# A decoder layer on one core: the order of work behind the last attention head

## The chip, the cores and the metric

The kernel runs on one core of a Trainium2 chip. The metric is the device time of one execution in microseconds (us), the median over runs. Its engines are TensorE (PE, matrix products, with PEld for its weight loads), VectorE (DVE), ScalarE (ACT), GpSimd (POOL) and SyncE (SP), which here only issues DMAs. They run side by side, each takes its own instructions in program order, and they meet through semaphores.

## The reference, cut to what matters

Batch 8, 128 rows each, width 512. Three blocks, each with a layer norm ahead and a residual behind:

```python
x = x + _L0_attn_ref(_layernorm(x), Wq, Wk, Wv, Wo)                      # causal self-attention, rope
x = x + _L0_xattn_ref(_layernorm(x), ctx_4096, Wq, Wk, Wv, Wo, qn, kn)   # 32 heads, 8 key heads of 128
x = x + _L0_ffn_ref(_layernorm(x), weight_q4, weight_scale, bias)        # one 512x512 product, 4-bit weights

# in _L0_xattn_ref
scores = jnp.einsum('bhgqd,bhkd->bhgqk', qg, k) * scale
probs = jax.nn.softmax(scores.astype(jnp.float32), axis=-1)
out = jnp.einsum('bhgqk,bhkd->bhgqd', probs, v)
...
return out @ Wo
```

## The kernel before

`self_attention` runs first and is not touched. `cross_attention_and_linear` runs the other two blocks. It goes through `STEPS` = 64 steps: key head j = 0 to 7 outside, batch row b = 0 to 7 inside, so step s is head s // 8 and row s % 8. Each step projects keys, values and queries of one row, takes the scores of the four query heads that share the key head, their softmax, the values, and adds the product with this head's slice of Wo to row b of `acc` (the residual stream, tile `x` in the trace). In the last head (j = `LAST` = 7) row b of `acc` is final after its step, so that the linear block's work on finished rows is spread over the steps that follow.

All products are split: a float32 operand is kept as a high part (rounded, `_hi`) and a low part (the rest, `_lo`), and `split_matmuls` issues for each slice three products: high x high, high x low and low x high (line 73). The high part is written by ACT (a copy that rounds), the low part by DVE or POOL (a subtraction), and before, a group of products starts when both parts stand.

The order of work is written out by hand, engine by engine, as calls of small functions that each wait for their semaphores and raise one. Names that matter, with s a step and b a row:

- SP: `probs_out(s)` writes the transposed blocks of the probabilities `p_blocks` to DRAM (L922), `probs_in(s)` reads them back as `pT_raw` in another layout (L930, four DMAs). The eight output rows are stored behind the loop over steps (L974); row b waits for `out_ok`.
- ACT: `probs_high(s)` rounds `pT_raw` into `pT_hi_sb` (L1113), `output_high(s)` rounds the attention output `ps_o` into `oT_hi` (L1124), `xn_high(b)` rounds the transposed normalised row `ps_xn` (L1135, tile `wkv_hi`).
- POOL: `probs_low(s)` subtracts (L1008), `row_rstd(b)` makes the layer norm's reciprocal deviation (L1027, L1029), `row_and_bias(b)` adds the bias to a row (L1037).
- DVE: `residual(s)` adds `ps_y` to `acc` (L1236), `statistics(b)` (L1259, L1261), `normalised(b)` (L1269, tile `raw_wkv`), `xn_low_row(b)` (L1274, tile `wkv_lo`), `output_low(s)` (L1240, tile `oT_lo`), `out_row(b)` adds the linear block's product and the biased row into `y` (L1284, tile `raw_wq`).
- PE: `values(s)` (tile `ps_o`, 6 products), `project_output(s)` (`ps_y`, 12 products), `xn_transposed(b)` (`ps_xn`, 4 transposes, L1396), `linear(b)` (12 products, into `ps_f` for even rows and `ps_q` for odd ones).

`y` has two buffers. `out_row(b)` from row 2 on waits until the store of row b - 2 has landed:

```python
if b >= 2:
    dve.wait_ge(stored[b % 2], 16 * (b // 2))
```

In the loop's last step (s = 63, b = 7) DVE ends with `residual(61)`, `statistics(5)` and `out_row(2)`. SP's program has by then `probs_out(63)` and `probs_in(63)` ahead of the first store.

Of the kernel before, what the change touches and what calls it, by code (L numbers as in the profile page):

```python
# [16 lines left out]
ALU = mybir.AluOpType  # L17
# [51 lines left out]
def split_matmuls(pe, out, parts, start=True, stop=True):  # L69

    terms = [(a, b) for lh, ll, rh, rl in parts for a, b in ((lh, rh), (lh, rl), (ll, rh))]
    for i, (lhsT, rhs) in enumerate(terms):
        mm = pe.matmul(out, lhsT, rhs, start=start and i == 0, stop=stop and i == len(terms) - 1)  # L73
    return mm


# [727 lines left out]
def cross_attention_and_linear(nc, mem, io):  # L804
# [7 lines left out]
    with ExitStack() as ctx:  # L812
# [83 lines left out]
        @block.sync  # L896
        def _(sp):
            def load(raw, name, sem, j):
                sp.dma_start(raw[:].rearrange("p c n -> p (c n)"), io[name][j]).then_inc(sem, 16)

            def queries_keys_out(s):

                sp.wait_ge(q_blocked, s + 1)
                sp.wait_ge(k_blocked, s + 1)
                wait(sp, qT_lo, s - 1)
                sp.dma_start(io["qk_scratch"][s % 2], qk_blocks[:].rearrange("p j x c -> p (j x c)")).then_inc(qk_stored, 16)

            def queries_keys_in(s):

                wait(sp, qT_lo, s - 1)  # L910
                wait(sp, kT_lo, s - 1)
                sp.wait_ge(qk_stored, 16 * (s + 1))
                quadrants = io["qk_scratch"][s % 2].rearrange("(i r) (j x) -> j r i x", i=4, j=4)
                for j in range(4):
                    sp.dma_start(qk_raw[s % 2][R * j:R * j + R].rearrange("p i x c -> p i (x c)"),
                                 quadrants[j]).then_inc(qk_loaded[s % 4], 16)

            def probs_out(s):

                sp.wait_ge(p_blocked, 2 * s + 2)  # L920
                wait(sp, pT_lo, s - 1)
                sp.dma_start(io["p_scratch"][s % 2], p_blocks[:].rearrange("p m g c -> p (m g c)")).then_inc(p_stored, 16)  # L922

            def probs_in(s):

                wait(sp, o_ps, s - 1)
                sp.wait_ge(p_stored, 16 * (s + 1))
                quadrants = io["p_scratch"][s % 2].rearrange("(i r) (j x) -> j r i x", i=4, j=4)
                for j in range(4):
                    sp.dma_start(f32(pT_raw[s % 2][R * j:R * j + R].rearrange("p i t x -> p i (t x)")),  # L930
                                 quadrants[j]).then_inc(p_loaded[s % 4], 16)

            def linear_scales(t):

                for g in range(8):
                    sp.dma_start(scale[16 * g:16 * g + 16, t, :],
                                 io["q4_scale"][8 * t + g:8 * t + g + 1, :].broadcast_to([16, D])).then_inc(scale_in, 16)

            queries_keys_out(0)
            queries_keys_in(0)  # L940
            load(raw_wkv, "x_wkv", wkv_in, 1)
            queries_keys_out(1)
            queries_keys_in(1)
            load(raw_wo, "x_wo", wo_in, 0)
            queries_keys_out(2)
            load(raw_wq, "x_wq", wq_in, 1)
            for s in range(STEPS):
                j, b = divmod(s, B)
                probs_out(s)
                if s + 2 < STEPS:  # L950
                    queries_keys_in(s + 2)
                probs_in(s)
                if s + 3 < STEPS:
                    queries_keys_out(s + 3)
                if b == 2 and j + 2 < XKVH:
                    sp.wait_ge(wkv_lo, 2 * j + 2)
                    load(raw_wkv, "x_wkv", wkv_in, j + 2)
                if b == 3 and j < LAST:
                    sp.wait_ge(wo_lo, j + 1)
                    load(raw_wo, "x_wo", wo_in, j + 1)  # L960
                if b == 5 and j + 2 < XKVH:
                    sp.wait_ge(wq_lo, 2 * j + 2)
                    load(raw_wq, "x_wq", wq_in, j + 2)
                if j + 1 == LAST:
                    if b == 5:
                        sp.wait_ge(wq_lo, 2 * LAST)
                        sp.dma_start(packed, io["q4"].rearrange("t p o -> p t o")).then_inc(packed_in, 16)
                        sp.dma_start(f_bias[:], io["bias"].broadcast_to([P, D])).then_inc(bias_in, 16)
                    if b >= 6:
                        linear_scales(b - 6)  # L970

            for b in range(B):
                sp.wait_ge(out_ok, b + 1)
                sp.dma_start(io["out"][b], y[:, b % 2, :]).then_inc(stored[b % 2], 16)  # L974
            for done in stored:
                sp.wait_ge(done, 16 * B // 2)

        @block.gpsimd
        def _(pool):
# [89 lines left out]
                        row_and_bias(b - 5)  # L1069
            row_rstd(5)  # L1070
            row_and_bias(3)
            probs_low(STEPS - 1)
            row_rstd(6)
            row_and_bias(4)
            row_and_bias(5)
# [5 lines left out]
        def _(act):  # L1081
# [92 lines left out]
            output_high(STEPS - 2)  # L1174
            xn_high(4)
            probs_high(STEPS - 1)
            xn_high(5)
            output_high(STEPS - 1)
            xn_high(6)
            xn_high(7)  # L1180

# [1 line left out]
        def _(dve):  # L1183
# [60 lines left out]
            def linear_bits(b):  # L1244
# [6 lines left out]
                if b in (1, 3):  # L1251
# [2 lines left out]
                    dve.wait_ge(scale_in, 16 * 16)  # L1254
                    dve.scalar_tensor_tensor(weights[h], bits[h], 2.0 / 15.0, scale, ALU.mult, ALU.mult).then_inc(product_ok, 1)

            def statistics(b):
                dve.wait_ge(acc_ok, LAST * B + b + 1)
                dve.bn_stats(stats[:, b, :], acc[:, b, :]).then_inc(stats_ok, 1)  # L1259
                dve.wait_ge(stats_ok, b + 1)  # L1260
                dve.bn_aggr(moments[:, b, :], stats[:, b, :]).then_inc(moments_ok, 1)  # L1261
# [30 lines left out]
            for s in range(STEPS):  # L1292
# [24 lines left out]
                if j == LAST:  # L1317
                    if b >= 2:
                        statistics(b - 2)
                    if b >= 5:  # L1320
                        out_row(b - 5)
            normalised(4)
            output_low(STEPS - 2)
            xn_low_row(4)
            normalised(5)
            out_row(3)
            residual(STEPS - 2)
            statistics(6)
            xn_low_row(5)
            normalised(6)  # L1330
            out_row(4)
            output_low(STEPS - 1)
            xn_low_row(6)
            residual(STEPS - 1)
            statistics(7)
            normalised(7)
            out_row(5)
            xn_low_row(7)
            out_row(6)
# [3 lines left out]
        def _(pe):  # L1343
# [38 lines left out]
            def project_output(s):  # L1382
# [4 lines left out]
                split_matmuls(pe, ps_y[:], [(oT[0][:, g, :], oT[1][:, g, :], wo[0][:, g, :], wo[1][:, g, :])  # L1387
                                            for g in range(XG)]).then_inc(y_ps, 1)

            def xn_transposed(b):  # L1390
                pe.wait_ge(xn_ok, b + 1)
                wait(pe, xn_lo, b)
# [41 lines left out]
            linear(3)  # L1434
            xn_transposed(4)
            project_output(STEPS - 2)
            xn_transposed(5)
            linear(4)
            values(STEPS - 1)
            xn_transposed(6)  # L1440
            project_output(STEPS - 1)
            linear(5)
            xn_transposed(7)
            linear(6)
            linear(7)


def build(nc, io):
# [65 lines left out]
```

## Time and profile before

| | us |
|---|---|
| time before, median of 3 runs | 992.04 |
| the 3 runs | 990.35, 992.80, 992.04 |
| span of the profiled execution, first to last instruction | 989.3 |
| PE busy | 927.3 (94%) |
| DVE busy | 742.3 (75%) |
| ACT busy | 604.4 (61%) |
| POOL busy | 568.9 (58%) |

The profiled execution is one of its own; its span is given, and what lies ahead of its first and behind its last instruction is not printed. The median of the runs stands 2.7 us above the span. A busy share is an average over the whole execution: PE is near full in the loop over steps, and in the last two of 40 slices its digit falls from 9 to 7. The views used are the chain of waits that ended last (each piece with its start and length, the engine and the tile it writes), and the timelines of single engines.

### The profile page before, as it was taken

The numbers are of one execution on the slowest core, as the hardware profiler recorded it, in microseconds if no ns is written. First come the engines' busy times: TensorE is split into PE (matmuls) and PEld (weight loads), VectorE is DVE, ScalarE is ACT, GpSimd is POOL, SyncE is SP. The second block draws the span as 40 slices with busy tenths as digits, with TensorE's granted clock in tenths as the row PEclk, the third lists the DMA queues.
The fourth block names the chain that finished last, engine by engine and source line by source line (L and its number), as shares of the span: only waits on it lengthen the run. The fifth ranks groups of instructions, "written<-read, shape, count | busy, mean of one in ns | idle before, by whom it ended". The sixth has DMA issues, their size and how long they took to land.

```text
span 989.3 us, 17511 instructions
## 1 busy us (share of the span) xinstructions
PE 927.3 (94%) x5484; PEld 797.2 (81%) x5492; DVE 742.3 (75%) x1555; ACT 604.4 (61%) x2226; POOL 568.9 (58%) x593
## 2 busy tenths in 40 slices
PE   5689999769999999999999999999999999999977
PEld 5567777548888888888888888888888888888765
DVE  6678988855877777777777777777777777789964
ACT  1568888615856676665667556765756675575530
POOL 6522322224865685677458656856774686468643
PEclk8799999779999999999999999999999999999999
DMA  5000020006666566557645665665576456654431
GB/s 203 12 12 13 12 87 12 1 1 223 211 219 205 168 209 208 172 167 231 211 149 186 213 210 169 198 209 178 167 236 196 150 175 209 214 170 150 134 117 54
DMA packets 101148, 149.84 MB, mean 151 GB/s; under 512 B 11840, under 2 KB 77376, under 8 KB 98880
## 3 DMA queue, kind: packets, MB, share of 16 engines
q1 hardware_dynamic: 101056, 148.71, 47.2%
q8 instruction: 45, 0.74, 0.3%
q14 instruction: 47, 0.39, 0.1%
HBM read 87.85 MB, written 60.82 MB: 150 GB/s over the span
## 4 chain that ended last, share of the span: by engine, by line
PE 69%; DVE 4%; ACT 1%; POOL 1%; issue 1%; DMA 1%; SPq 0%; DVEq 0%; POOLq 0%
PE ps_kv L73 17%; PE ps_y L73 17%; PE ps_q L73 17%; PE ps_o L73 8%; PE ps_s L73 8%; ACT ps_s L1090 1%; DVE p L1202 1%; PE ps_f L73 1%; DVE neg_max L1190 1%; POOL pT_raw L1008 1%; DVE p_blocks L1206 0%; DVE raw_wkv L1269 0%; DMA out<-raw_wq 0%; DVE kT_lo L1229 0%; DVE f_stats L1259 0%
## 5 line engine op out<-in xcount | busy, mean ns | idle before, releaser
L1090 ACT ACTIVATE ps_s<-ps_s,bias,q_rms 128x256 f32<-128x256 f32 x256 | 136.8, 535 | 139.5 <-DVE bias L1194 139.5
L1001 POOL TENSOR_TENSOR qT_lo<-qk_raw,qT_hi 128x512 fp32r<-128x512 f32 x64 | 84.6, 1322 | 202.6 <-ACT qT_hi L1119 202.6
L1008 POOL TENSOR_TENSOR pT_raw<-pT_raw,pT_hi_sb 128x1024 fp32r<-128x1024 f32 x64 | 154.1, 2408 | 11.9 <-ACT pT_hi_sb L1113 11.6
L1107 ACT ACTIVATE q_squares<-ps_q 128x128 bf16<-128x128 f32 x256 | 67.5, 278 | 112.0 <-DVE qk_blocks L1224 112.0
L73 PE MATMUL ps_y<-wo_hi,oT_hi 128*128 128x512 f32 x256 | 101.7, 397 | 4.9 <-DVE oT_lo L1240 4.9
L73 PE MATMUL ps_q<-wq_lo,xT_hi 128*128 128x512 f32 x256 | 101.4, 396 | 0.0
L73 PE MATMUL ps_q<-wq_hi,xT_lo 128*128 128x512 f32 x256 | 101.1, 395 | 0.0
L73 PE MATMUL ps_y<-wo_lo,oT_hi 128*128 128x512 f32 x256 | 101.1, 395 | 0.0
L1206 DVE STREAM_TRANSPOSE p_blocks<-p 128x512 f32<-128x512 f32 x128 | 91.1, 711 | 13.3
L73 PE MATMUL ps_y<-wo_hi,oT_lo 128*128 128x512 f32 x256 | 101.0, 394 | 0.0
L73 PE MATMUL ps_q<-wq_hi,xT_hi 128*128 128x512 f32 x256 | 100.9, 394 | 0.0
L1236 DVE TENSOR_TENSOR x<-ps_y,x 128x512 f32<-128x512 f32 x64 | 44.2, 691 | 70.4 <-PE ps_y L73 70.3
L1202 DVE TENSOR_TENSOR p<-ps_s,inv 128x512 f32<-128x512 f32 x128 | 88.6, 692 | 4.4
L1190 DVE TENSOR_REDUCE neg_max<-ps_s 128x2 f32<-128x512 f32 x128 | 87.7, 685 | 5.3
L73 PE MATMUL ps_kv<-wkv_hi,cT_hi 128*128 128x256 f32 x256 | 73.7, 288 | 4.1 <-DVE k_sb L1214 4.1
L1224 DVE STREAM_TRANSPOSE qk_blocks<-ps_q 128x512 f32<-128x512 f32 x64 | 45.8, 716 | 42.2 <-PE ps_q L73 41.9
L73 PE MATMUL ps_s<-kT_hi,qT_hi 128*128 128x256 f32 x256 | 72.6, 284 | 2.7 <-DVE kT_lo L1229 1.3
L73 PE MATMUL ps_kv<-wkv_hi,cT_lo 128*128 128x256 f32 x256 | 73.2, 286 | 0.0
L73 PE MATMUL ps_kv<-wkv_lo,cT_hi 128*128 128x256 f32 x256 | 73.1, 286 | 0.0
L73 PE MATMUL ps_kv<-wkv_hi,xT_hi 128*128 128x256 f32 x256 | 73.0, 285 | 0.0
L73 PE MATMUL ps_kv<-wkv_lo,xT_hi 128*128 128x256 f32 x256 | 72.6, 284 | 0.0
L73 PE MATMUL ps_kv<-wkv_hi,xT_lo 128*128 128x256 f32 x256 | 72.5, 283 | 0.0
(217 smaller groups left out, 2940.2 us busy)
## 6 DMA issues: line engine op xcount, KB each, us to landing
p_scratch<-p_blocks SPq DMA_DIRECT2D x64, 512.0 KB, 3.0
pT_raw<-p_scratch SPq DMA_DIRECT2D x256, 128.0 KB, 3.1
qk_scratch<-qk_blocks SPq DMA_DIRECT2D x64, 384.0 KB, 3.5
qk_raw<-qk_scratch SPq DMA_DIRECT2D x256, 96.0 KB, 2.9
raw_wq<-in_x_wq SPq DMA_DIRECT2D x8, 1024.0 KB, 7.8
raw_wo<-in_x_wo SPq DMA_DIRECT2D x8, 1024.0 KB, 7.5
raw_wkv<-in_x_wkv SPq DMA_DIRECT2D x8, 512.0 KB, 5.0
ctx_raw<-in_ctxT SPq DMA_DIRECT2D x8, 256.0 KB, 2.7
```

Source lines behind the costliest of these rows:

```text
L73: mm = pe.matmul(out, lhsT, rhs, start=start and i == 0, stop=stop and i == len(terms) - 1)
L1001: pool.tensor_tensor(qT[1][:].rearrange("p g (i c) -> p g i c", i=4), qk_raw[s % 2][:, :, 0:XG, :].rearrange("p i g c -> p g i c"), f32(qT ...
L1008: pool.tensor_tensor(raw, f32(raw), f32(pT_hi_sb[:].rearrange("p i t x -> p (i t x)")), ALU.subtract).then_inc(pT_lo, 1)
L1090: e = act.activation(scores, scores, ACT.Exp, bias=bias[:, g:g + 1], scale=q_rms[:, s % 4, g:g + 1], accum_out=total[:, g:g + 1])
L1107: i = act.activation(q_squares[:, g, :], ps_q[:, g * XD:(g + 1) * XD], ACT.Square, scale=XD ** -0.5, accum_out=q_mean[:, g:g + 1])
L1190: dve.tensor_reduce(neg_max[:, two], ps_s[h][:].rearrange("p (g k) -> p g k", g=2), AX.X, ALU.max, negate=True).then_inc(max_ok, 1)
L1202: dve.tensor_tensor(p[:, two, :], ps_s[h][:].rearrange("p (g k) -> p g k", g=2), inv[:, two].unsqueeze(2).broadcast_to([P, 2, KV]), ALU.mu ...
L1206: dve.transpose(p_blocks[:, :, two, :], p[:, two, :].rearrange("p g (m r) -> p m g r", r=R)).then_inc(p_blocked, 1)
L1224: dve.transpose(qk_blocks[:, :, 0:XG, :].rearrange("p j x c -> p x j c"), ps_q[:].rearrange("p (g j r) -> p g j r", g=XG, r=R)).then_inc(q ...
L1236: dve.tensor_tensor(acc[:, b, :], ps_y[:], acc[:, b, :], ALU.add).then_inc(acc_ok, 1)
```

## The change

Four edits, all in the last head.

1. SP: the store of rows 0 and 1 moves into the loop, to the head of steps 62 and 63; rows 2 to 7 are stored behind it.
2. PE: the products of the last step with values and with Wo, and the linear product of row 7, are issued with the products of the high part first, which wait for the high part alone; the products of the low part wait for it and come last. The count of products is unchanged.
3. `probs_low(63)`, the low part of the last probabilities, moves from POOL to DVE.
4. Behind the loop the calls are put in another order on PE, DVE and ACT.

```diff
+def high_parts_first(pe, out, parts, low, count, start=True, stop=True):
+
+    for i, (lh, _, rh, rl) in enumerate(parts):
+        pe.matmul(out, lh, rh, start=start and i == 0, stop=False)
+        pe.matmul(out, lh, rl, start=False, stop=False)
+    pe.wait_ge(low, count)
+    for i, (_, ll, rh, _) in enumerate(parts):
+        mm = pe.matmul(out, ll, rh, start=False, stop=stop and i == len(parts) - 1)
     return mm
@@ sync
+            def store(b):
+                sp.wait_ge(out_ok, b + 1)
+                sp.dma_start(io["out"][b], y[:, b % 2, :]).then_inc(stored[b % 2], 16)
...
                 j, b = divmod(s, B)
+                if j == LAST and b >= 6:
+                    store(b - 6)
                 probs_out(s)
...
-            for b in range(B):
-                sp.wait_ge(out_ok, b + 1)
-                sp.dma_start(io["out"][b], y[:, b % 2, :]).then_inc(stored[b % 2], 16)
+            for b in range(2, B):
+                store(b)
@@ gpsimd
             row_and_bias(3)
-            probs_low(STEPS - 1)
             row_rstd(6)
@@ scalar
             probs_high(STEPS - 1)
+            output_high(STEPS - 1)
             xn_high(5)
-            output_high(STEPS - 1)
             xn_high(6)
@@ vector
+            def probs_low(s):
+                dve.wait_ge(pT_hi, s + 1)
+                raw = pT_raw[s % 2][:].rearrange("p i t x -> p (i t x)")
+                dve.tensor_tensor(raw, f32(raw), f32(pT_hi_sb[:].rearrange("p i t x -> p (i t x)")),
+                                  ALU.subtract).then_inc(pT_lo, 1)
...
+            output_low(STEPS - 2)
             normalised(4)
-            output_low(STEPS - 2)
             xn_low_row(4)
             normalised(5)
+            probs_low(STEPS - 1)
             out_row(3)
             residual(STEPS - 2)
+            output_low(STEPS - 1)
             statistics(6)
             xn_low_row(5)
             normalised(6)
             out_row(4)
-            output_low(STEPS - 1)
-            xn_low_row(6)
             residual(STEPS - 1)
             statistics(7)
             normalised(7)
+            xn_low_row(6)
             out_row(5)
@@ tensor
+            def last_values():
+                s = STEPS - 1
+                pe.wait_ge(pT_hi, s + 1)
+                pe.wait_ge(o_lo, s)
+                hi, lo = pT_hi_sb, pT_raw[s % 2]
+                for t in range(2):
+                    for x in range(2):
+                        pe.matmul(ps_o[:], v[s % 5][x][:, t, :], hi[:, :, t, :], start=t == 0 and x == 0, stop=False)
+                pe.wait_ge(pT_lo, s + 1)
+                for t in range(2):
+                    mm = pe.matmul(ps_o[:], v[s % 5][0][:, t, :], lo[:, :, t, :], start=False, stop=t == 1)
+                mm.then_inc(o_ps, 1)
+
+            def last_output():
+                pe.wait_ge(o_hi, STEPS)
+                pe.wait_ge(acc_ok, STEPS - 1)
+                high_parts_first(pe, ps_y[:], ..., o_lo, STEPS).then_inc(y_ps, 1)
+
+            def last_linear():
+                pe.wait_ge(xn_hi, B)
+                pe.wait_ge(out_ok, B - 2)
+                x = xnT[(B - 1) % 2]
+                high_parts_first(pe, ps_f[(B - 1) % 2][:], ..., xn_lo, B).then_inc(f_ps, 1)
...
             project_output(STEPS - 2)
+            last_values()
             xn_transposed(5)
             linear(4)
-            values(STEPS - 1)
+            last_output()
+            linear(5)
             xn_transposed(6)
-            project_output(STEPS - 1)
-            linear(5)
+            linear(6)
             xn_transposed(7)
-            linear(6)
-            linear(7)
+            last_linear()
```

SP's queue at its end, before; `out_0` is the output in DRAM, `p_scratch` and `pT_raw` the round trip of the probabilities of steps 62 and 63:

```order
L922 DMA p_scratch0<-p_blocks 128x1024 [waits pT_lo,p_blocked]
L930 DMA pT_raw0<-p_scratch0 32x4x256 [waits p_stored,b_o_ps]
L930 DMA pT_raw0<-p_scratch0 32x4x256 x3
L922 DMA p_scratch1<-p_blocks 128x1024 [waits pT_lo,p_blocked]
L930 DMA pT_raw1<-p_scratch1 32x4x256 [waits p_stored,b_o_ps]
L930 DMA pT_raw1<-p_scratch1 32x4x256 x3
L974 DMA out_0<-raw_wq 128x512 [waits f_out_ok] x8
```

All eight stores stand behind both round trips.

The same place of SP's queue in the changed kernel:

```order
L952 DMA out_0<-raw_wq 128x512 [waits f_out_ok]
L933 DMA p_scratch0<-p_blocks 128x1024 [waits pT_lo,p_blocked]
L941 DMA pT_raw0<-p_scratch0 32x4x256 [waits p_stored,b_o_ps]
L941 DMA pT_raw0<-p_scratch0 32x4x256 x3
L952 DMA out_0<-raw_wq 128x512 [waits f_out_ok]
L933 DMA p_scratch1<-p_blocks 128x1024 [waits pT_lo,p_blocked]
L941 DMA pT_raw1<-p_scratch1 32x4x256 [waits p_stored,b_o_ps]
L941 DMA pT_raw1<-p_scratch1 32x4x256 x3
L952 DMA out_0<-raw_wq 128x512 [waits f_out_ok] x6
```

One store stands ahead of each of the two round trips, six behind.

DVE before, from `out_row(2)`, the last call of the loop, to `output_low(63)`:

```order
L1284 TENSOR_TENSOR raw_wq<-ps_f,raw_wq 128x512 [waits stored_even,f_base_ok,f_ps]
L1269 TENSOR_SCALAR raw_wkv<-x,f_moments,f_rstd 128x512 [waits f_xT_ps,f_rstd_ok]
L1240 TENSOR_TENSOR oT_lo<-ps_o,oT_hi 128x512 [waits b_o_hi]
L1274 TENSOR_TENSOR wkv_lo<-ps_xn,wkv_hi 128x4x128 [waits f_xn_hi]
L1269 TENSOR_SCALAR raw_wkv<-x,f_moments,f_rstd 128x512 [waits f_xT_ps,f_rstd_ok]
L1284 TENSOR_TENSOR raw_wq<-ps_q,raw_wq 128x512 [waits stored_odd,f_base_ok,f_ps]
L1236 TENSOR_TENSOR x<-ps_y,x 128x512 [waits b_y_ps]
L1259 BN_STATS f_stats<-x 128x6 [waits b_acc_ok]
L1261 BN_AGGR f_moments<-f_stats 128x2 [waits f_stats_ok]
L1274 TENSOR_TENSOR wkv_lo<-ps_xn,wkv_hi 128x4x128 [waits f_xn_hi]
L1269 TENSOR_SCALAR raw_wkv<-x,f_moments,f_rstd 128x512 [waits f_xT_ps,f_rstd_ok]
L1284 TENSOR_TENSOR raw_wq<-ps_f,raw_wq 128x512 [waits stored_even,f_base_ok,f_ps]
```

`output_low(63)` is the next row behind these. The same stretch in the changed kernel:

```order
L1305 TENSOR_TENSOR raw_wq<-ps_f,raw_wq 128x512 [waits stored_even,f_base_ok,f_ps]
L1255 TENSOR_TENSOR oT_lo<-ps_o,oT_hi 128x512 [waits b_o_hi]
L1290 TENSOR_SCALAR raw_wkv<-x,f_moments,f_rstd 128x512 [waits f_xT_ps,f_rstd_ok]
L1295 TENSOR_TENSOR wkv_lo<-ps_xn,wkv_hi 128x4x128 [waits f_xn_hi]
L1290 TENSOR_SCALAR raw_wkv<-x,f_moments,f_rstd 128x512 [waits f_xT_ps,f_rstd_ok]
L1275 TENSOR_TENSOR pT_raw1<-pT_raw1,pT_hi_sb 128x1024 [waits pT_hi]
L1305 TENSOR_TENSOR raw_wq<-ps_q,raw_wq 128x512 [waits stored_odd,f_base_ok,f_ps]
L1251 TENSOR_TENSOR x<-ps_y,x 128x512 [waits b_y_ps]
L1255 TENSOR_TENSOR oT_lo<-ps_o,oT_hi 128x512 [waits b_o_hi]
```

`probs_low(63)` (L1275) is new here, and `output_low(63)` (the last row) follows `residual(62)` directly.

DVE at its very end, before, from `output_low(63)` on:

```order
L1240 TENSOR_TENSOR oT_lo<-ps_o,oT_hi 128x512 [waits b_o_hi]
L1274 TENSOR_TENSOR wkv_lo<-ps_xn,wkv_hi 128x4x128 [waits f_xn_hi]
L1236 TENSOR_TENSOR x<-ps_y,x 128x512 [waits b_y_ps]
L1259 BN_STATS f_stats<-x 128x6 [waits b_acc_ok]
L1261 BN_AGGR f_moments<-f_stats 128x2 [waits f_stats_ok]
L1269 TENSOR_SCALAR raw_wkv<-x,f_moments,f_rstd 128x512 [waits f_xT_ps,f_rstd_ok]
L1284 TENSOR_TENSOR raw_wq<-ps_q,raw_wq 128x512 [waits stored_odd,f_base_ok,f_ps]
```

The changed kernel from `residual(63)` on:

```order
L1251 TENSOR_TENSOR x<-ps_y,x 128x512 [waits b_y_ps]
L1280 BN_STATS f_stats<-x 128x6 [waits b_acc_ok]
L1282 BN_AGGR f_moments<-f_stats 128x2 [waits f_stats_ok]
L1290 TENSOR_SCALAR raw_wkv<-x,f_moments,f_rstd 128x512 [waits f_xT_ps,f_rstd_ok]
L1295 TENSOR_TENSOR wkv_lo<-ps_xn,wkv_hi 128x4x128 [waits f_xn_hi]
L1305 TENSOR_TENSOR raw_wq<-ps_q,raw_wq 128x512 [waits stored_odd,f_base_ok,f_ps]
```

`xn_low_row(6)` stood ahead of `residual(63)`; now it stands behind `normalised(7)`.

## Rows read from the trace of the kernel before

**Rows 1.** the page's head

```profile
span 989.3 us, 17511 instructions
```

**Rows 2.** the chain of waits from 952 us: start, length, engine, tile

```profile
952.68 2.62 DMA p_scratch<-p_blocks
...
956.65 0.43 SPq L930
...
957.13 3.24 DMA out<-raw_wq
...
961.10 0.55 DVE raw_wkv L1269
...
961.69 0.75 PE ps_xn L1396 x4
962.44 2.92 PE ps_y L73 x12
965.35 0.47 PE ps_xn L1396 x4
965.82 2.79 PE ps_f L73 x12
968.61 1.40 PE ps_o L73 x6
...
970.03 0.61 ACT oT_hi L1124
...
971.41 3.08 PE ps_y L73 x12
...
974.51 0.70 DVE x L1236
...
977.15 1.49 DVE raw_wkv L1269
...
978.68 0.75 PE ps_xn L1396 x4
979.43 2.77 PE ps_f L73 x12
982.19 2.73 PE ps_q L73 x12
...
984.95 0.69 DVE raw_wq L1284
```

**Rows 3.** PE's timeline, the last product of linear(3)

```profile
958.25 0.39 PE L73 MATMUL ps_q<-wq_hi,wkv_lo 128*128 128x512 f32 x1
```

**Rows 4.** DVE's timeline: start, length, line, tiles; in brackets the idle time ahead

```profile
930.35 2.49 DVE L1229 SCALAR_TENSOR_TENSOR kT_lo<-qk_raw,key_scale,kT_hi 128x256 fp32r<-128x256 f32 x1
...
945.77 0.69 DVE L1284 TENSOR_TENSOR raw_wq<-ps_q,raw_wq 128x512 f32<-128x512 f32 x1 [0.80 <-POOL raw_wq L1037]
...
955.64 0.18 DVE L1261 BATCH_NORM_AGGREGATE f_moments<-f_stats 128x2 f32<-128x6 f32 x1
960.49 0.69 DVE L1284 TENSOR_TENSOR raw_wq<-ps_f,raw_wq 128x512 f32<-128x512 f32 x1 [4.66 <-DMA out<-raw_wq]
...
978.54 0.68 DVE L1284 TENSOR_TENSOR raw_wq<-ps_q,raw_wq 128x512 f32<-128x512 f32 x1
```

**Rows 5.** POOL's timeline, two places

```profile
930.18 2.38 POOL L1008 TENSOR_TENSOR pT_raw<-pT_raw,pT_hi_sb 128x1024 fp32r<-128x1024 f32 x1 [0.29 <-ACT pT_hi_sb L1113]
...
956.76 1.29 POOL L1037 TENSOR_TENSOR raw_wq<-x,f_bias 128x512 f32<-128x512 f32 x1
```

**Rows 6.** DMA issues of the read-back, 955.3 to 957.1: KB each, median us to landing

```profile
pT_raw<-p_scratch SPq DMA_DIRECT2D x4, 128.0 KB, 3.1
```

**Rows 7.** ACT's timeline, probs_high(63)

```profile
962.97 1.05 ACT L1113 ACTIVATE pT_hi_sb<-pT_raw 128x1024 fp32r<-128x1024 f32 x1
```

**Rows 8.** one line's instructions: least, median, most ns; line 504, self-attention

```profile
L504 DVE TENSOR_TENSOR wq_lo<-raw_wq,wq_hi x2: 1215/1220/1226, 10.1 to 16.2; 128x1024 fp32r<-128x1024 f32 x2
```

**Rows 9.** one tile's instructions, the same columns: kT_lo

```profile
L1229 DVE SCALAR_TENSOR_TENSOR kT_lo<-qk_raw,key_scale,kT_hi x64: 443/469/2489, 232.0 to 941.7; 128x256 fp32r<-128x256 f32 x64
```

More of the change, by code:

```diff
@@ L73, in split_matmuls @@
         mm = pe.matmul(out, lhsT, rhs, start=start and i == 0, stop=stop and i == len(terms) - 1)
+    return mm
+def high_parts_first(pe, out, parts, low, count, start=True, stop=True):
[5 more added lines that the diff above has]
+        mm = pe.matmul(out, ll, rh, start=False, stop=stop and i == len(parts) - 1)
     return mm
@@ L1388, in project_output @@
                                             for g in range(XG)]).then_inc(y_ps, 1)
+            def last_values():
[13 more added lines that the diff above has]
+                pe.wait_ge(acc_ok, STEPS - 1)
+                high_parts_first(pe, ps_y[:], [(oT[0][:, g, :], oT[1][:, g, :], wo[0][:, g, :], wo[1][:, g, :])
+                                               for g in range(XG)], o_lo, STEPS).then_inc(y_ps, 1)
+            def last_linear():
+                pe.wait_ge(xn_hi, B)
+                pe.wait_ge(out_ok, B - 2)
+                x = xnT[(B - 1) % 2]
+                high_parts_first(pe, ps_f[(B - 1) % 2][:], [(x[0][:, c, :], x[1][:, c, :], w[0][:, c, :], w[1][:, c, :])
+                                                            for c in range(C)], xn_lo, B).then_inc(f_ps, 1)
             def xn_transposed(b):
```

## The prediction

> **What bounds the kernel now.** The span is 989.3 us [rows 1]; the median of the runs, 992.04, stands 2.7 us above it, and I carry that difference over unchanged: the sum is made on the span, then taken off the median. All that the change touches lies behind 930 us, so I read the chain of waits there [rows 2], then the engines' timelines at the places where it leaves PE. The reader is to see that over the last 30 us PE no longer sets the pace alone. `linear(3)` ends at 958.25 + 0.39 = 958.64 [rows 3], and PE's next piece, `xn_transposed(4)`, starts at 961.69 [rows 2]: 3.05 us of nothing. It waits for `normalised(4)` (961.10 [rows 2]), which stands on DVE behind `out_row(2)`, and that waited 4.66 us for a store [rows 4]: `out_row(2)` needs row 0 stored, and SP issued this store only at 957.13, behind the last read-back of the probabilities [rows 2], though row 0 was ready long before. A second gap is before `project_output(63)`: `values(63)` ends at 970.01, the 12 products start at 971.41, in between ACT's and DVE's split of `ps_o` (PE fills part of it with one set of transposes) [rows 2]. From 974.51 to 978.68 PE waits, but for one linear row, on residual, statistics and `normalised(7)`, and then 0.75 + 2.77 + 2.73 us of PE and `out_row(7)` at 984.95 end the chain [rows 2].
>
> **The stores.** With row 0 stored in step 62, `out_row(2)` starts when `statistics(5)` leaves DVE: 955.64 + 0.18 = 955.82 instead of 960.49 [rows 4], 4.67 us earlier. What is late next? `output_low(62)` now follows it, and then `normalised(4)`, at about 955.8 + 0.7 + 0.7 = 957.2. POOL adds a bias row from 956.76 to 958.05 [rows 5], and the normalising instruction is 0.55 us in one place and 1.49 in another [rows 2]. Bounds: 957.75 alone, 958.7 with the long form. PE is busy to 958.64 either way, so the price is between nothing and 0.1; I take nothing. So all 3.05 us of the gap go.
>
> PE from there, end to end by the chain's pieces [rows 2]:
>
> 958.64, `xn_transposed(4)` 0.47, `project_output(62)` 2.92: 962.03. `last_values` 1.40: 963.43. `xn_transposed(5)` 0.47, `linear(4)` 2.79: 966.69. `last_output` 2.77: 969.46.
>
> Then `residual(63)` starts at 969.5 instead of 974.51: 5.0 us earlier. It is more than 3.05 because `linear(4)` now fills the time in which `ps_o` is split (1.4 us before), because transposes and products without a standstill ahead cost 0.47 and 2.77 instead of 0.75 and 3.08 [rows 2], and because `xn_transposed(6)` has moved behind.
>
> **Do the inputs arrive?** The last read-back DMA is issued at 956.65 [rows 2] and takes 3.1 us to land [rows 6], so 959.75. `xn_high(4)` leaves ACT at about 959.7, so `probs_high(63)` runs from 959.75 for 1.05 us [rows 7], to 960.8. PE wants it at 962.03: 1.2 us of cover. `probs_low(63)` on DVE: the trace has the same form (128x1024, two tiles in SBUF, the same types) in the self-attention at 1.22 us [rows 8], against 2.38 on POOL [rows 5]. So the low part is there at 962.1, and `last_values` needs it after four of its six products, at 962.03 + 0.93 = 962.96: 0.85 us of cover. On POOL it would be there at 963.2, some 0.3 late, so this edit is worth 0 to 0.3. `output_high(63)` then ends at 963.43 + 0.61 = 964.06, the low part 0.75 later at 964.8, both well before 966.69. So putting the high parts first costs and gains nothing in `last_output`; what helped was `linear(4)` in between.
>
> The stored rows' own DMAs: one issue of some 0.4 us each on SP, which otherwise waits there. Row 1 is in `y` at 945.77 + 0.69 = 946.46 [rows 4] and SP's next issue, of the probabilities, is at 952.68 [rows 2], 6.2 us later, against 3.24 us from issue to landing of a store [rows 2]; step 62 has the same order. No cost.
>
> **The tail pays something back.** From `residual(63)` to `normalised(7)`'s start is 974.51 to 977.15, 2.64 us [rows 2]: now 969.5 to 972.12. DVE gives over to the next instruction at 978.54 [rows 4], 1.39 us after that start: 973.51. There the new order has `xn_low_row(6)` (0.7 and a semaphore, 0.74: 974.25), and `linear(6)` waits for it. PE has ended `linear(5)` and `xn_transposed(6)` by 969.46 + 2.79 + 0.47 = 972.7 and stands for 1.5 us. Then `linear(6)` from standstill 3.08 (977.33), `xn_transposed(7)` 0.47 (977.80), ACT's `xn_high(7)` 0.61 and semaphores (978.45), `last_linear` from standstill 3.08 (981.53), `out_row(7)` at 981.55. Before, transposes, `linear(6)` and `linear(7)` ran without a gap and covered the split of row 7. Here high parts first does save something: `last_linear` waits for ACT alone, 0.7 us less than for DVE's part. From `residual(63)` to `out_row(7)` it is 12.05 us against 10.44: 1.6 us go back.
>
> **Sum:** 984.95 - 981.55 = 3.4 us. Span 985.9, time 992.04 - 3.4 = 988.6.
>
> **Rivals.**
>
> (a) *The low part on DVE collides with POOL.* Where both worked on SBUF, DVE lost: `kT_lo`, 0.47 us in the median, took 2.49 from 930.35 [rows 4, 9] while POOL subtracted from 930.18 for 2.38 [rows 5]. If POOL's bias row (1.29 us [rows 5]) ran just ahead of `probs_low(63)`, the low part would be there at 963.4 instead of 962.1, PE would wait 0.45 us, and a read-back that landed late as well would add up to about 0.5. Gain 2.4 to 2.9, time 989.1 to 989.6. Against it: that row is over by 958.05 [rows 5], 2.8 us before, and POOL's next work waits for `statistics(6)`, which stands behind `probs_low(63)` on DVE.
>
> The Trainium skill, SBUF — State Buffer, section "Who interferes with whom", says that a DVE instruction with two SBUF inputs contends with a GpSimd instruction that reads SBUF, and that the second one is held up entirely; by that rule, which the 2.49 us bears out, the move is safe only while POOL stands still, and the sum would be 989.1 if it did not.
>
> (b) *The tail gives back more, or all is within noise.* The tail's 1.6 us contains four ends read from other places, each good to 0.1 or 0.2, and `linear(6)` might also be held by `xn_high(6)` (972.7 + 0.65 = 973.4, 0.1 us of cover only). With 2.2 us given back the gain is 2.8, 989.2.
>
> (c) *The tail gives back nothing,* since the gaps of 1.5 and 0.65 us on PE shrink: then the whole 5.0 us of the earlier `residual(63)` stay, 987.0.
>
> (d) *Slower: the stores block SP.* SP takes its queue in order. If it reached the store before the row is in `y`, or if the round trip's packets waited for the store's, each of steps 62 and 63 would lose up to 3.24 us to landing and 0.4 to issue, 7.3 in all: 992.04 - 3.4 + 7.3 = 995.9. It decides from the point where the row is ready less than about 3.6 us before the probabilities; it is 6.2 here. Its `out_row` also stands ahead of that step's probabilities on DVE.
>
> (e) *It doesn't do what it says:* `out_row(2)` finds another late input, its bias row. POOL makes this before the one at 956.76, so the wait ends by 956.8 at the latest, and `normalised(4)` by about 959: 0.3 us, gain 3.1, inside the forecast's range.
>
> **How the numbers follow.** About 0.3% (3.0 us) is what a measurement of this kernel can tell from no change. The forecast (gain 3.0 to 4.1, with e) has 0.55; (c) and what lies towards it 0.08; (a) 0.10 and (b) 0.20, both gains of 2 to 3 us; something that eats the gain to within a us 0.03; (d) 0.04. Faster: 0.55 + 0.08 = 0.63, less 0.01 for the spread of runs (990.35 to 992.8): 0.62. Slower: 0.04. Same: the rest, 0.34. The range: from (c) less a small spread, 986.7, to (a) and (b) with a us of spread, 990.6; outside are (d) and the worst of the rest.
>
> **What would show it.** Right: no wait for a store at `out_row(2)`, which starts near 955.8 if the span up to there is equal; PE without a gap from `linear(3)` to `linear(5)`; `residual(63)` 5 us earlier; `probs_low(63)` at 1.22 us; PE standing about 1.5 us ahead of `linear(6)` and 0.65 ahead of `last_linear`. Wrong: a gap inside `last_values` (a), a wait longer than 2 us ahead of `linear(6)` (b), or the read-backs of steps 62 and 63 landing later than 4 us (d).

## The result, and the profile after

The changed kernel takes 986.45 us (median of 11 runs, 982.41 to 988.46), the kernel before 991.22 in 11 runs beside it (987.08 to 994.52). The ratio is 0.9946 [0.9928, 0.9964] (in brackets the 95% interval), a gain of 5.4 us with 1.8 on either side; the two medians differ by 4.8. The forecast was 988.6 in a range from 986.7 to 990.6. So the direction was right and the time lies 0.25 us below the range: the kernel gained more than the sum said. The profiled span went from 989.3 to 984.4 us.

First the place at which the change aims. DVE's timeline of the changed kernel (start, length, line, operation, tiles; in brackets the idle time ahead and who ended it):

```profile
955.48 0.18 DVE L1282 BATCH_NORM_AGGREGATE f_moments<-f_stats 128x2 f32<-128x6 f32 x1
955.59 0.69 DVE L1305 TENSOR_TENSOR raw_wq<-ps_f,raw_wq 128x512 f32<-128x512 f32 x1
...
956.98 1.19 DVE L1290 TENSOR_SCALAR raw_wkv<-x,f_moments,f_rstd 128x512 f32<-128x512 f32 x1
...
960.70 1.22 DVE L1275 TENSOR_TENSOR pT_raw<-pT_raw,pT_hi_sb 128x1024 fp32r<-128x1024 f32 x1
```

`out_row(2)`, which waited 4.66 us for a store [rows 4], now starts 0.11 us behind the start of the last instruction of `statistics(5)`, with nothing in brackets. The third row is `normalised(4)`, the last the low part of the probabilities on its new engine: 1.22 us, as the row of the self-attention had said [rows 8].

Next the chain of waits of the changed kernel from `linear(3)` on (start, length, engine, tile, line):

```profile
955.71 2.73 PE ps_q L73 x12
958.44 0.53 PE ps_xn L1444 x4
958.97 2.80 PE ps_y L73 x12
961.78 0.93 PE ps_o L1419 x4
962.71 0.47 PE ps_o L1422 x2
963.18 0.47 PE ps_xn L1444 x4
963.65 2.77 PE ps_f L73 x12
966.42 0.24 PE ps_y L80
...
968.28 0.94 PE ps_y L84 x4
...
969.25 0.70 DVE x L1251
...
971.89 1.29 DVE raw_wkv L1290
...
973.29 0.69 DVE wkv_lo L1295
...
974.02 3.03 PE ps_f L73 x12
977.05 0.48 PE ps_xn L1444 x4
...
977.56 0.61 ACT wkv_hi L1150
...
978.21 0.50 PE ps_q L80
...
981.26 0.69 DVE raw_wq L1305
```

Each PE piece begins where the one above ends, from 955.71 to 969.22. The 3.05 us gap and the gap ahead of `project_output(63)` [rows 2] are gone. Then comes what the tail gives back: `linear(6)` starts at 974.02, behind the chain of residual, statistics, `normalised(7)` and `xn_low_row(6)`, and `last_linear` at 978.21, behind ACT's `xn_high(7)`. PE's timeline has the two gaps in brackets:

```profile
974.02 0.50 PE L73 MATMUL ps_f<-wq_hi,wkv_hi 128*128 128x512 f32 x1 [1.58 <-DVE wkv_lo L1295]
...
978.21 0.50 PE L80 MATMUL ps_q<-wq_hi,wkv_hi 128*128 128x512 f32 x1 [0.69 <-ACT wkv_hi L1150]
```

What no step of the forecast covered lies behind `out_row(7)`: before, the span ends 989.3 - 984.95 = 4.35 us after that instruction starts [rows 1, 2]; now it is 984.4 - 981.26 = 3.14.

**A ruler.** Whole runs of one program lie up to 9 us apart (987.0 to 996.5 us for the kernel before, over all sets). The spread is there before the stages that the change touches: the first residual sum of the self-attention starts at 66.0 to 71.4 us in the fourteen profiles, and that does not go by kernel (68.45 and 70.26 in two executions of before, 70.16 and 66.03 in two of after). From there to the last instruction of `statistics(5)` another 885.1 to 888.0 us pass, and that does not go by kernel either (887.19 and 885.37, 885.32 and 885.78 in the same four). So I measure each profile from the start of the last instruction of `statistics(5)`, which the change leaves in place, to the end of the span. Two executions of after agree on this stretch within 0.07 us. What follows on the differences between variants rests on this ruler, with three profiles of before, two of after and one of each other kernel: the intervals of the timed ratios, 1.7 to 2.6 us on either side, are too wide to tell most of the variants from each other. In the table all lengths are us; "rest" is from the start of `out_row(7)` to the end of the span; "gap" is PE's standstill behind `linear(3)`.

| profile | statistics(5) to residual(63) | to out_row(7) | rest | sum | gap |
|---|---|---|---|---|---|
| before | 18.87 | 10.44 | 4.35 | 33.66 | 3.05 |
| before, second execution (a0) | 20.28 | 10.46 | 4.33 | 35.07 | 2.96 |
| before, third execution (a2) | 18.87 | 10.44 | 4.32 | 33.63 | 3.07 |
| after | 13.77 | 12.01 | 3.14 | 28.92 | none |
| after, second execution (a1) | 13.77 | 12.00 | 3.22 | 28.99 | none |
| e1, stores alone | 15.41 | 10.46 | 4.38 | 30.25 | none |
| e2, all but the stores | 19.21 | 11.99 | 3.22 | 34.42 | 3.66 |
| e3, row 6 split early | 13.79 | 10.15 | 3.14 | 27.08 | none |
| e4, row 7 inside linear(6) | 13.78 | 9.21 | 3.15 | 26.14 | none |
| e5, low part on POOL | 14.52 | 12.03 | 4.36 | 30.91 | none |
| e6, no high parts first | 14.24 | 12.73 | 3.18 | 30.15 | none |
| e7, e1 and two DVE instructions | 15.43 | 10.44 | 3.15 | 29.02 | none |
| e8, before with PE kept busy | 18.80 | 10.43 | 4.40 | 33.63 | 0.65 |
| e9, e2 with PE kept busy | 17.72 | 12.05 | 3.14 | 32.91 | 1.36 |

### The profile page after: what moved, and what is told of

Read it like the earlier page. It is cut to its first block, busy times and chain, and to the rows that moved or that the text cites. A ratio compares the mean times of both kernels' runs of the same rounds, so it can differ in the third digit from the quotient of the medians.

```text
span 984.4 us, 17519 instructions
## 1 busy us (share of the span) xinstructions
PE 926.3 (94%) x5492; PEld 795.9 (81%) x5492; DVE 744.0 (76%) x1556; ACT 604.3 (61%) x2226; POOL 565.4 (57%) x592
## 4 chain that ended last, share of the span: by engine, by line
PE 70%; DVE 3%; ACT 2%; POOL 1%; DMA 1%; issue 0%; SPq 0%; DVEq 0%; POOLq 0%
PE ps_kv L73 17%; PE ps_y L73 17%; PE ps_q L73 17%; PE ps_o L73 8%; PE ps_s L73 8%; POOL pT_raw L1024 1%; PE ps_f L73 1%; ACT ps_s L1105 1%; DVE p L1217 0%; DVE neg_max L1205 0%; DVE p_blocks L1221 0%; DMA p_scratch<-p_blocks 0%; DMA pT_raw<-p_scratch 0%; ACT pT_hi_sb L1128 0%; DVE f_stats L1280 0%
## 5 line engine op out<-in xcount | busy, mean ns | idle before, releaser
L1024 POOL TENSOR_TENSOR pT_raw<-pT_raw,pT_hi_sb 128x1024 fp32r<-128x1024 f32 x63 | 151.7, 2408 | 5.9 <-ACT pT_hi_sb L1128 5.5
L73 PE MATMUL ps_s<-kT_hi,qT_lo 128*128 128x256 f32 x256 | 72.4, 283 | 0.0
L73 PE MATMUL ps_s<-kT_lo,qT_hi 128*128 128x256 f32 x256 | 72.3, 283 | 0.0
```

The lines of the kernel that those rows point to most:

```text
L1024: pool.tensor_tensor(raw, f32(raw), f32(pT_hi_sb[:].rearrange("p i t x -> p (i t x)")), ALU.subtract).then_inc(pT_lo, 1)
```

## The experiments

The theories, by the letters that the expectations use. **A:** the stretch up to `out_row(7)` is worth about 3.5 us as forecast, and the rest is chance. **B:** one to two us more are real, and lie behind `out_row(7)` or ahead of step 60. **C:** the new order is worth something of its own, beside the stores. Two more came up with the first results: **D:** what the last store waits for is a fetch of instructions, whose time DVE's program sets. **E:** PE's clock falls after its standstill in some executions, so the standstill costs more than its length.

### Both kernels again: a0, a1

No edit. 

> The kernel before once more, unchanged, beside itself: what two sets of runs of one program differ by, and a second profile. Theory A (the change is worth the 3.5 us that the stretch from linear(3) to out_row(7) shows, the rest of the 4.9 us between the two profiled spans is chance): from the start of out_row(7) to the end of the span, 4.35 us in the first profile, may come out anywhere between 3.1 and 4.4; ratio 1.000. Theory B (1 to 2 us more are real, behind the last out_row or ahead of step 60): again 4.3 us behind out_row(7), and out_row(2) within 0.3 us of 960.5.

> The changed kernel once more. Theory A: out_row(7) 3.5 us earlier than in the new profile of before when both are laid on the same step 60; 2.4 us (first profile: 3.1 from out_row(7) to the end) may grow to 4.3; ratio between 0.9955 and 0.9975 (2.5 to 4.5 us). Theory B: 3.1 us from out_row(7) to the end again, ratio 0.993 to 0.9955 (4.5 to 7 us).

Before gave 991.62 us (12 runs), 1.001 [0.9992, 1.0027] of the kernel before; after gave 986.44 (12 runs), 0.9954 [0.9935, 0.9974], a gain of 4.6 us. So the two medians repeat within 0.4 us. The rest behind `out_row(7)` repeats too: 4.33 and 3.22. It belongs to the program, which speaks for B and against A. The profile of a0 held something new, 1.41 us more ahead of `residual(63)`. Its granted clock around the standstill (one row for each stretch: from and to, length, busy time and count of PE, PEld, DVE, ACT and POOL, granted clock, DMA share, GB/s):

```profile
958.50:961.50 3.00, 0.12 (x1) 0.00 (x0) 1.12 (x3) 0.00 (x0) 0.00 (x0) 1.00 0.56 191
962.50:966.20 3.70, 3.70 (x11) 2.87 (x10) 1.75 (x3) 1.41 (x2) 2.22 (x1) 0.54 0.20 75
966.20:970.00 3.80, 3.80 (x20) 3.23 (x19) 2.69 (x5) 0.60 (x1) 1.54 (x4) 1.00 0.03 10
```

PE does next to nothing for 3 us, starts again at 961.58, and is then granted 0.54 over 3.7 us, about the lower of its two levels (1.2 of 2.4 GHz), though it is busy throughout. In the first profile of before, the same place shows 1.00:

```profile
962.60:966.30 3.70, 3.70 (x19) 3.08 (x18) 2.62 (x5) 1.86 (x3) 2.21 (x1) 1.00 0.20 75
```

In a0's chain of waits `project_output(62)` is the piece that pays, 4.46 us where [rows 2] has 2.92:

```profile
962.33 4.46 PE ps_y L73 x12
```

### The stores alone, and all but the stores: e1, e2

e1 is before with

```
+    if j == LAST and b >= 6:
+        store(b - 6)
     probs_out(s)
...
-for b in range(B):
+for b in range(2, B):
```

and nothing else; e2 is the changed kernel with these two places as in before.

> Only the stores of rows 0 and 1 move into the loop; order, engines and products as before. Theory A: out_row(2) starts with the end of statistics(5), near 955.8; PE's 3.05 us ahead of xn_transposed(4) go, the 1.4 us between values(63) and project_output(63) stay (0.9 of it idle), the tail stays 10.4 us: residual(63) 3.3 us earlier, time 3.3 us less than before, as much as the whole change by my sum. A rival, C, in which the reordering is worth something of its own: 1 to 2 us less than the change gains.

> The whole change without the stores' move: out_row(2) waits for the store of row 0 again. Theory A: out_row(2) at 960.4, output_low(62) now ahead of normalised(4), so xn_transposed(4) at 962.3, 0.6 later than before; linear(4) in the gap of ps_o and fewer standstills take back 1.7, so residual(63) about 1.1 us earlier than before; the tail 1.6 longer; in all 0 to 0.5 us slower than before. Rival C: 1 to 2 us faster.

e1 gave 985.42 us (12 runs), 0.9951 [0.9933, 0.9969]; e2 gave 988.38 (12 runs), 0.9996 [0.9977, 1.0016]. On the ruler e1 gains 3.41 us on before, and the whole change gains 4.74, of which 1.21 are the rest behind `out_row(7)`: 3.53 without it. So nearly all of the stretch's gain is the stores'. The timed runs don't tell e1 (0.9951) from the whole change (0.9946 and 0.9954). The rest of the change speeds up the middle by 15.41 - 13.77 = 1.64 and gives 12.01 - 10.46 = 1.55 back in the tail. The chain of e1 shows how little the old order leaves to win once the standstill is gone:

```profile
956.05 0.47 PE ps_xn L1401 x4
956.52 2.80 PE ps_y L73 x12
959.32 0.47 PE ps_xn L1401 x4
959.78 2.78 PE ps_f L73 x12
962.57 1.40 PE ps_o L73 x6
...
965.37 3.07 PE ps_y L73 x12
...
968.46 0.70 DVE x L1241
```

PE runs gapless to 963.97; from there to `residual(63)` it stands only 0.94 of the 1.40 us in which `ps_o` is split, to 965.37. C falls for the stretch. But e1's rest is 4.38 and e2's is 3.22: what is won behind `out_row(7)` comes with the part of the change that is not the stores. And e2, with the standstill (3.66 us of it), has the slow products too: `project_output(62)` takes 4.15 us in its chain. It had been expected 0 to 0.5 us slower than before; on the ruler it is 0.76 slower, with the slow products in it and 1.13 us given back behind `out_row(7)`.

### Parts of the tail moved further: e3, e4

e3 is after with row 6 split one place earlier, so that `linear(6)` needs nothing of row 7:

```
 last_output()
-linear(5)
 xn_transposed(6)
+linear(5)
 linear(6)
...
+xn_low_row(6)
 normalised(7)
-xn_low_row(6)
 out_row(5)
```

e4 is e3 with the transposes of row 7 between the two halves of `linear(6)`:

```
-linear(6)
-xn_transposed(7)
+linear(6, between=lambda: xn_transposed(7))
```

> The changed kernel with the transposes of row 6 ahead of linear(5), and xn_low_row(6) ahead of normalised(7) on DVE. Theory A: the 1.58 us that PE stands ahead of linear(6) goes, since the low part of row 6 is ready while linear(5) runs; from residual(63) to out_row(7): 0.47 + 2.79 + 2.79 + 0.47 + 0.65 + 3.08 = 10.25 us against 12.01 in the changed kernel, 1.75 us less. Rival: normalised(7) is delayed by the DVE instruction now ahead of it and the transposes of row 7 become late: 0.7 us or less gained.

> As e3_row6_early, and the transposes of row 7 stand between the two halves of linear(6), so that the second half covers ACT's copy of row 7. Theory A: from residual(63) to out_row(7) 0.47 + 2.79 + 1.4 + 0.47 + 1.4 + 2.75 = 9.3 us, 2.7 less than in the changed kernel, about 8 us less than before in all. Rival: ACT's or DVE's part of row 7 is late by up to 0.7, gain 2.0.

e3 gave 981.61 us (6 runs), 0.9905 [0.9879, 0.9931]; e4 984.55 (6 runs), 0.9924 [0.9898, 0.9949]. On the ruler e3 is 1.84 shorter than after and e4 2.78. The chain of e4 ends without any gap on PE:

```profile
970.50 0.47 PE ps_xn L1444 x4
970.97 2.79 PE ps_q L73 x12
973.76 1.37 PE ps_f L73 x6
975.12 0.47 PE ps_xn L1444 x4
975.59 1.39 PE ps_f L73 x6
976.98 0.23 PE ps_q L80
...
979.75 0.69 DVE raw_wq L1305
```

e3 loses the first of the tail's two gaps and e4 both, each with PE's restart behind it, so the 1.55 us given back was a matter of order alone. Both kernels beat before clear of their intervals. That they beat after is the ruler's word: their intervals overlap that of after. Which of the two is the faster as a whole six runs don't tell, and the medians lie the other way; the ruler says e4 by 0.94.

### Two parts of the change undone: e5, e6

e5 is after with the last low part back on POOL; e6 is after with plain products in place of the three functions that take the high parts first:

```
 row_and_bias(3)
+probs_low(STEPS - 1)      (e5, POOL; on DVE the line goes)
...
-last_values()   last_output()                last_linear()     (e6, PE)
+values(STEPS - 1)   project_output(STEPS - 1)   linear(7)
```

> The changed kernel with the last probabilities' low part on POOL again. For the stretch: POOL's subtraction (2.4 us) starts at the end of probs_high(63) and ends some 0.3 us after PE has issued the four products of the high part, so PE waits 0.3 and out_row(7) is 0 to 0.4 us later. For the end, theory D (the last store lands 1.2 us earlier in the changed order because an instruction fetch, which in the old order runs while it lands, comes earlier; DVE's program decides, by one instruction): DVE has an instruction less here, so the fetch falls on the last store again and it lands in 3.2 us instead of 2.0. Rival: the fetch is PE's or comes with the order of work, and the store lands in 2.0 us.

> The changed kernel with plain order of products in the last step's three groups: each waits for both parts. Theory A: last values 0 (the low part is there 0.85 us ahead of its first need, but now needed 0.93 earlier: up to 0.2 us of wait), project_output(63) 0, linear(7) 0.7 us later since it waits for DVE's part of row 7. Out_row(7) 0.7 to 0.9 us later than in the changed kernel. The last store lands in 2.0 us (theory D: DVE's program is that of the changed kernel).

e5 and e6 gave 988.41 and 988.44 us (10 runs each), both 0.9964 [0.9943, 0.9984]. On the ruler e5 loses 0.75 ahead of `residual(63)`, and PE's timeline has the wait that the forecast had put at 0 to 0.3:

```profile
964.21 0.73 PE L1422 MATMUL ps_o<-pT_raw,v_hi 128*128 128x512 f32 x2 [0.48 <-POOL pT_raw L1024]
```

The two products that need the low part come 0.48 us late and then take 0.73 us in the chain instead of 0.47, longer behind a wait as the twelve products of [rows 2] were (3.08 against 2.77). e6 loses 0.47 ahead of `residual(63)` and 0.72 in the tail. Its waits of PE from 955 us on (engine, tile and line, waited for what: total us, times, longest):

```profile
PE ps_q L73 <- DVE wkv_lo L1295: 1.4, 1, 1.4
PE ps_o L73 <- DVE pT_raw L1275: 0.2, 1, 0.2
```

The first is `linear(7)`, which stands 1.4 us where `last_linear` stood 0.69: the saving of 0.7 that the forecast gave it. The second is `values(63)`, which waits 0.20 us for the low part ahead of its first product; its six products then take 1.67 us in the chain instead of 1.40, and the two make the 0.47. Both kernels lose more up to `out_row(7)` than had been expected of them: 0.77 us against 0 to 0.4, and 1.19 against 0.7 to 0.9.

e5 also showed where the rest comes from. It runs the same products as after, DVE has one instruction less, and the rest is 4.36 again. The table sorts by that count: the six profiles in which DVE has as many instructions as in before have a rest of 4.32 to 4.40 us, the eight with one or two more 3.14 to 3.22.

### The end of the span: e7

e7 is e1 with two small instructions on DVE that nothing depends on:

```
+for two in (slice(0, 2), slice(2, 4)):
+    dve.reciprocal(inv[:, two], total[:, two])
 out_row(6)
```

> e1_stores_alone with two tiny instructions more on DVE (reciprocals of two columns, whose result nobody reads) ahead of out_row(6), where DVE waits 1.4 us anyway. Theory D: DVE's program reaches the point that starts the instruction fetch earlier, so the fetch is over before the last store and it lands in 2.0 us instead of 3.2: 3.1 to 3.2 us from out_row(7) to the end instead of 4.4, out_row(7) itself unmoved (25.9 us behind statistics(5)'s last instruction). Rival: the fetch belongs to another engine, the store lands in 3.2 us and the end stays 4.4 us behind.

It gave 983.65 us (8 runs), 0.9949 [0.9923, 0.9975]. The two instructions lie in time in which DVE waits anyway, and `out_row(7)` does not move (10.44 against 10.46), but the rest falls from 4.38 to 3.15. SP's wait for the last store, in before, e1, e5, after and e7, in this order:

```profile
SPq L976 <- DMA out<-raw_wq: 2.8, 1, 2.8
```
```profile
SPq L981 <- DMA out<-raw_wq: 2.9, 1, 2.9
```
```profile
SPq L992 <- DMA out<-raw_wq: 2.9, 1, 2.9
```
```profile
SPq L992 <- DMA out<-raw_wq: 1.7, 1, 1.7
```
```profile
SPq L981 <- DMA out<-raw_wq: 1.7, 1, 1.7
```

It is the same store of 256 KB every time. The DMA view of before, of 985.6 to 985.8 us (the issue: KB, us to landing), and of 987.4 to 987.6, 1.8 us later (a queue: packets, MB, share of 16 engines):

```profile
out<-raw_wq SPq DMA_DIRECT2D x1, 256.0 KB, 3.2
```
```profile
q14 instruction: 1, 0.01, 9.7%
```

And of after, of 981.9 to 982.1 us, and of 979.1 to 979.6:

```profile
out<-raw_wq SPq DMA_DIRECT2D x1, 256.0 KB, 2.0
```
```profile
q14 instruction: 2, 0.02, 8.4%
```

With a packet of the instruction queue in the store's landing time it lands in 3.2 us, with the packets ahead of it in 2.0. In e5 the packet comes at 985.4 to 985.7, behind the store of 983.8, and it takes 3.2; in e7 at 976.2 to 976.5, ahead of the store of 978.4, and it takes 2.0. So D holds: two instructions on DVE moved the fetch and took 1.2 us off the end, with PE's work and `out_row(7)` where they were. The timed runs can't show it (0.9949 against 0.9951 for e1).

The last five stores of all fourteen profiles, 70 in all, sort without exception. Where no packet of the instruction queue runs among the store's own packets, in 56 of them, the store lands in 2.0 us; where one does, in 14, it takes 2.5 to 3.7. In these 14 too, 15 of a store's 16 landings come at 2.0 us and the last alone is late. At the end of before one can see how: the packet of the instruction queue runs from 987.50 to 987.81, a last packet of 4 bytes of the store starts at 987.81, 0.49 us behind the others of its kind, and the last landing is at 988.85, 1.18 us behind the fifteenth. Why that packet takes 1.04 us from its start to its landing, where the last of the others takes 0.35, is not shown.

### The standstill filled: e8, e9, a2

e8 is before and e9 is e2, both with ten products behind `linear(3)` whose results nobody reads; a2 is before once more, one run.

```
 linear(3)
+pe.wait_ge(p_ok, 2 * STEPS)
+for _ in range(10):
+    pe.matmul(ps_s[0][:], xT[0][:, 0, 0:S], wo[0][:, 0, :], start=True, stop=True)
```

> The kernel before with ten products between linear(3) and xn_transposed(4) that nobody reads: 2.3 us of the 3.05 in which PE stands. Theory E (PE's clock falls to its lower level for some 4 us, after the standstill, in some executions, and takes 1.4 us): no fall here, the granted clock is 1.00 throughout, project_output(62) takes 2.8 to 2.9 us, and statistics(5) to the end is 33.3 to 33.7 us. Rival: the fall has nothing to do with the standstill and comes in this kernel too: 4.2 to 4.5 us for project_output(62), 35 us.

> e2_all_but_stores with the same ten products, 2.3 us of the 3.7 in which PE stands there. Theory E: no fall of the clock, project_output(62) 2.8 to 2.9 us instead of 4.15, statistics(5) to the end 33.1 us instead of 34.42. Rival: the fall comes all the same, 34.4 us.

> The kernel before, a third profile. Theory E: from statistics(5) to the end either 33.7 us (clock 1.00 behind the standstill) or 35.1 (a fall to the lower level), nothing between; the last store lands in 3.2 us in either case.

e8 gave 988.79 us (8 runs), 0.9991 [0.9969, 1.0013]; e9 989.49 (8 runs), 0.9974 [0.9951, 0.9997]; a2 993.09. In neither e8 nor e9 did the clock fall: `project_output(62)` takes 2.92 and 2.81 us in their chains. In a2, though, it did not fall either (2.92), behind a standstill of 3.07 us. Over all fourteen profiles, from 900 us to the end of PE's work: with a standstill of about 3 us or more (2.96 to 3.66) the clock fell in two of four, a0 and e2; without, or with the standstill cut to 1.36 or less, in none of ten. So E holds as far as that the fall is seen only behind the long standstill and costs about 1.4 us where it comes. That the standstill causes it is not shown: at two falls in four, two kernels like e8 and e9 would both go without one by chance one time in four. What decides in which executions it comes stays open: 2.96 us was enough in a0, 3.05 and 3.07 were not in before and a2. How often it comes in the timed runs can't be read from their times, and e8, which should be faster than before on average, does not show it outside its interval.

## Why the prediction was right, and where it fell short

**Right: the stores.** `out_row(2)` waits for nothing and PE's gap is gone, as forecast; `residual(63)` starts 18.87 - 13.77 = 5.10 us earlier, against 5.0. e1 has the mechanism by itself. The input that was to be late next, `normalised(4)`, took 1.19 us, between the two forms of 0.55 and 1.49, and PE's transposes followed `linear(3)` directly: the price of nothing that was taken stands. The Trainium skill, SBUF — State Buffer, section "Who interferes with whom", says that DVE's `tensor_scalar` can enter modes that use the pair of ports it shares with GpSimd, when its operands meet certain conditions, and that whichever of the two issues first has the pair for its whole instruction and blocks the other. The trace agrees as far as the blocking: `normalised(4)` started 0.39 us into POOL's bias row (956.59 to 957.89) and ended 0.28 us behind its end, the same form took 0.54 us from 960.25 with POOL idle, and the low part, with POOL idle too, took 1.22 as in [rows 8].

**Right: the tail.** 10.44 became 12.01, 1.57 us back against 1.6, with PE's gaps of 1.58 and 0.69 us against 1.5 and 0.65. The sum up to `out_row(7)` is 5.10 - 1.57 = 3.53 us against 3.4. Rivals (a), (b), (d) and (e) did not come (for (d): the read-backs behind the two stores land in 2.9 and 3.0 us), nor did (c), although its 987.0 is nearer to the measured time than the forecast: the tail did give 1.6 back, and what makes up for it lies elsewhere.

**Wrong: the sum that ends at `out_row(7)`.** "984.95 - 981.55 = 3.4 us. Span 985.9" takes the piece behind that instruction over from before, 4.35 us, without a term; it was 3.14. That is 1.21 us of the miss, decided by when the last fetch of instructions runs, and so by how many instructions DVE has (e5, e7). The trace of before showed the fetch 1.8 us behind the issue of the last store and this store landing in 3.2 us; I read neither.

**Wrong: the point that it was taken off**, "I carry that difference over unchanged". The median of three runs, 992.04, was 0.82 us above the median of 11, 991.22. Every run whose span is on record stands 1.7 to 1.8 us above it; the 2.7 also held how far the profiled execution lay from the median. In the larger sets median less span is 1.92 and 2.05. With 1.21 and the 0.13 by which the stretch gained more, the 0.82 makes the 2.15 us between 988.6 and 986.45 to within rounding, all of it on one side; either of the two larger terms alone would have left the time inside the range. That it fits so closely is partly luck, since the measured gain is good to 1.8 us only.

**Missing: the clock behind the standstill.** The sum prices the gap at its length. Where the clock fell it cost 1.4 us more, so the change removes 3.5 + 1.2 = 4.7 us in executions without a fall, and 6.1 in those with one. The measured 4.6 and 5.4 us, with 1.8 to 1.9 on either side, fit both and don't tell the shares.

**Undersized: two small edits.** The low part on DVE was put at 0 to 0.3 us and is worth 0.75 ahead of `residual(63)` in the new order: the delay was 0.48, and PE's restart comes on top. It is also the edit that gives DVE its additional instruction, so the 1.22 us by which e5's end is longer (4.36 against 3.14) are its doing too. High parts first in the values was not given a price; e6 puts it at 0.47.

## What to carry to other kernels

Where a row of a buffer waits for its last store, look at what stands ahead of that store in the issuing queue: moving two issues was 3.4 of the 4.7 us here, and the reorder around it won in the middle what it lost in the tail, until the tail was ordered as well (e3, e4). When a sum is made on a chain, give the piece behind its last computing instruction a term of its own, with the DMA that lands there and what else moves at that moment. And when the runs spread more than the effect, measure each profile from the last instruction that the change leaves alone: here that repeats within 0.1 us, but for the execution in which the clock fell, where the ratios of the timed runs are good to 2 us.

## What the runs showed of the chip

A store among whose packets one of the instruction queue ran landed late: the last one in 3.2 us instead of 2.0, others in 2.5 to 3.7, with 15 of 16 landings on time. Two instructions that do nothing useful moved it and made the kernel's end 1.23 us shorter (4.38 to 3.15).

TensorE's clock fell to about its lower level (0.54 granted) after the engine had stood for 3 us and gone back to work, in two of four executions. PE was fully busy all that time; the products start 0.43 us apart at the lower level (a0, 963 to 966 us) instead of 0.23, and the clock is at 1.00 again from 966.2 us on.

The first 70 us of the same program differ by up to 4 us between executions (70.16 and 66.03 in after), and the granted clock there differs as well: from 18 to 21 us it was 0.50 in a0, as in after, and 1.00 in a1. The two are not at the same work by then, as PE's busy time shows. The rows of a0 and a1:

```profile
18.00:21.00 3.00, 3.00 (x8) 2.42 (x9) 0.40 (x1) 0.00 (x0) 0.00 (x0) 0.50 0.66 191
```
```profile
18.00:21.00 3.00, 0.76 (x7) 0.52 (x5) 2.94 (x11) 1.28 (x2) 2.42 (x4) 1.00 0.66 270
```

What starts this difference was not tried.
